# Moving the statistics of chunks three and four into the feed-forward loop of an audio tower on one core

## The reference

```python
h = tok(x)                                              # projection, dynamic convolution, feed-forward, residual
h = h + attn(layernorm(h), w_qkv, b_qkv, w_o, b_o)      # out = vals @ w_o.T + b_o
h = h + ffn(layernorm(h), up, down, perm)
```

## Time and profile before

| what | value |
|---|---|
| median of 3 runs | 1031.34 us |
| time of the profiled execution | 1035.96 us |
| its span, first to last instruction | 1034.2 us |
| mean granted TensorE clock | 0.977 of full |
| PE busy | 967.4 us (94%) |
| DVE, ACT, POOL busy | 509.2, 424.4, 394.3 us |
| DMA, mean over the span | 121 GB/s |

### The profile page before, as it was taken

How to read it: one execution, slowest core, us unless ns; L and a number is a source line. 1 busy time by engine, 2 the same in 40 slices (tenths; PEclk the granted TensorE clock), 3 DMA queues, 4 the chain that set the end, 5 groups by cost and what they waited for, 6 DMA issues and landing times.

```text
span 1034.2 us, 15644 instructions
## 1 busy us (share of the span) xinstructions
PE 967.4 (94%) x6108; PEld 714.5 (69%) x6108; DVE 509.2 (49%) x848; ACT 424.4 (41%) x753; POOL 394.3 (38%) x317
## 2 busy tenths in 40 slices
PE   7999999987899999999879999999999999889996
PEld 5777777776777788778657877877887777323331
DVE  6153535659447502254756256256064567755551
ACT  6144444555433533434243243243132332356553
POOL 1225252227601122723361451451023377748532
PEclk9999999999899999999989999999999999899998
DMA  8542725395343154327100201200214975533421
GB/s 290 209 165 4 205 7 181 4 285 203 117 145 107 62 126 164 109 95 265 41 11 22 92 11 35 79 11 22 92 52 149 289 260 209 184 111 133 149 77 61
DMA packets 75062, 124.96 MB, mean 121 GB/s; under 512 B 29159, under 2 KB 38375, under 8 KB 70894
## 3 DMA queue, kind: packets, MB, share of 16 engines
q1 hardware_dynamic: 68830, 107.03, 33.7%
q0 software_dynamic: 5120, 16.78, 4.6%
q10 hardware_dynamic: 1040, 0.16, 0.1%
HBM read 81.46 MB, written 42.50 MB: 120 GB/s over the span
## 4 chain that ended last, share of the span: by engine, by line
PE 53%; issue 10%; POOL 7%; DVE 5%; DMA 3%; ACT 2%; another core or an unknown queue 1%; POOLq 0%; SPq 0%; DVEq 0%; ACTq 0%
PE bank L299 14%; PE bank L301 13%; PE bank L300 13%; PE bank L1795 3%; PE bank L1804 3%; POOL vacc L335 2%; PE bank L1551 1%; POOL out L758 1%; POOL acc L363 1%; DVE sq L377 1%; DMA stage<-w_qkv_t 1%; POOL acc L308 1%; DVE acc L1219 1%; PE bank L1523 1%; DMA db_late<-h_s 1%
## 5 line engine op out<-in xcount | busy, mean ns | idle before, releaser
L335 POOL TENSOR_TENSOR vacc<-vacc,sq 128x512 f32<-128x512 f32 x72 | 97.2, 1350 | 45.8 <-ACT sq L381 36.4
L299 PE MATMUL bank<-xa_h,wp_h 128*128 128x512 f32 x256 | 103.4, 404 | 7.2 <-DVE xa_l L1094 7.2
L299 PE MATMUL bank<-cv_h,wf_h 128*128 128x512 f32 x256 | 106.3, 415 | 1.2 <-POOL wf_l L293 1.2
L301 PE MATMUL bank<-cv_h,wf_l 128*128 128x512 f32 x256 | 101.4, 396 | 0.0
L300 PE MATMUL bank<-cv_l,wf_h 128*128 128x512 f32 x256 | 101.4, 396 | 0.0
L300 PE MATMUL bank<-xa_l,wp_h 128*128 128x512 f32 x256 | 101.1, 395 | 0.0
L301 PE MATMUL bank<-xa_h,wp_l 128*128 128x512 f32 x256 | 101.1, 395 | 0.0
L700 POOL TENSOR_TENSOR fo<-fo,res 128x512 f32<-128x512 f32 x32 | 43.5, 1373 | 123.4 <-ACT fo L837 89.8
L1077 ACT ACTIVATE gt<-bank 128x512 f32<-128x512 f32 x128 | 66.2, 600 | 39.0 <-PE bank L1795 36.8
L1795 PE MATMUL bank<-dd,up_f 64*128 64x512 f32 x256 | 67.9, 651 | 5.6 <-ACT gt L1077 5.4
L381 ACT ACTIVATE sq<-sq 128x512 f32<-128x512 f32 x56 | 35.1, 632 | 79.3 <-DVE sq L377 79.3
(11 more groups left out here) (179 smaller groups left out, 2167.5 us busy)
## 6 DMA issues: line engine op xcount, KB each, us to landing
xs<-x_t SPq DMA_DIRECT2D x32, 256.0 KB, 6.2
h_s<-ho SPq DMA_DIRECT2D x8, 1024.0 KB, 5.9
res<-h_s SPq DMA_DIRECT2D x32, 256.0 KB, 3.6
h_s<-fo SPq DMA_DIRECT2D x32, 256.0 KB, 2.4
dc<-h_s SPq DMA_DIRECT2D x4, 2048.0 KB, 9.3
h<-h_s SPq DMA_DIRECT2D x8, 1024.0 KB, 10.5
h_s<-h SPq DMA_DIRECT2D x8, 1024.0 KB, 4.8
stage<-w_qkv_t SPq DMA_DIRECT2D x24, 256.0 KB, 3.6
```

Source lines behind the costliest of these rows:

```text
L299: pe.matmul(o, wh, xh, start=start, stop=False)
L301: return pe.matmul(o, wl, xh, start=False, stop=stop)
L335: g.tensor_tensor(vacc[:, :], t[:, 0, :] if k == 1 else vacc[:, :], t[:, k % 2, :], ALU.add).then_inc(ln_pool, 1)
```

## The change

The centres, squares, adds and the variance product of chunk three (number 2) leave the output projection of chunk four and go into the feed-forward loop: its centres into steps 0 to 3, two a step, its variance product behind step 5, its root behind the gelus of step 6. Those of chunk four go into steps 7 to 12 (one, two, one, two, one, one), its variance product behind step 14. The mean product of chunk four moves from step 1 to step 5, its copy from step 2 to step 6. Both variance products now write into bank 7. In the last output-projection chunk DVE runs `d_prep` of chunk one's blocks 0 to 3, moves banks 0 to 2 out, runs `d_prep` of blocks 4 to 7, and goes on with the other banks. `d_prep` of the later chunks starts at step 4 and not 3. In every projection chunk `o_sum` now stands ahead of the last low-part split of the next chunk. SP stores chunk three's reciprocal after `d_stat_load(1)`. The one counter `ln_pool` (14 a statistic) is split into `ln_sum` and `ln_vac` (7 each), so that sums and adds of different chunks can interleave; this renames waits and changes no count that they stand for (the hunks with renames alone are left out).

```diff
@@ -169,8 +169,8 @@
-        ln_pool, ln_mean, ln_d, ln_sq, ln_var, ln_std, ln_rstd = (
-            sem(s) for s in ("ln_pool", "ln_mean", "ln_d", "ln_sq", "ln_var", "ln_std", "ln_rstd"))
+        ln_sum, ln_vac, ln_mean, ln_d, ln_sq, ln_var, ln_std, ln_rstd = (
+            sem(s) for s in ("ln_sum", "ln_vac", "ln_mean", "ln_d", "ln_sq", "ln_var", "ln_std", "ln_rstd"))
...
@@ -638,12 +638,13 @@
                                  h2[c % 2][:, 4 * g:4 * g + 4, :]).then_inc(o_st[c % 2][g], 16)
                 if c > 0 and c + 1 < CH:
                     h2_load(c + 1)
-                if c > 0:
+                if 0 < c < CH - 1:
                     stat_store(CH + c - 2, 1)
                 if c == 1:
                     d_stat_load(0)
 
             d_stat_load(1)
+            stat_store(2 * CH - 3, 1)
             d_stat_load(2)
             stat_store(2 * CH - 2, 0)
             stat_store(2 * CH - 2, 1)
@@ -766,14 +767,16 @@
                     gather(0, range(4))
                 if c == 3:
                     gather(0, range(4, KB))
-                ln_var_pool(g, 2 * CH + c - 1)
+                if c < CH - 1:
+                    ln_var_pool(g, 2 * CH + c - 1)
                 o_sum(c)
 
             gather(1)
             for s in range(CH * KB + 1):
-                k = s - STAT_FROM
-                if 0 < k < KB:
-                    ln_var_add(g, 3 * CH - 1, k)
+                for i, steps in enumerate(CENTERS):
+                    for k in steps.get(s - 1, ()):
+                        if k > 0:
+                            ln_var_add(g, 3 * CH - 2 + i, k)
                 if s > 0:
                     scatter((s - 1) // KB, (s - 1) % KB)
                 n, k = divmod(s - GATHER_AFTER, KB)
@@ -1059,11 +1062,11 @@
                     if c == 1:
                         act.wait_ge(vo_st, 64 * CH)
                     stat_copy_act(act, L, CH + c - 2)
-                    for k in range(KB):
+                    for k in range(KB if c < CH - 1 else 0):
                         stat_square_act(act, L, k)
                 if c + 1 < CH:
                     vs_high(c + 1, range(PAIRS - 1))
-                if c > 0:
+                if 0 < c < CH - 1:
                     stat_std_act(act, L, VAR_BANK)
                 if c + 1 < CH:
                     vs_high(c + 1, [PAIRS - 1])
@@ -1079,12 +1082,14 @@
             L = 3 * CH - 1
             for s in range(CH * KB):
                 gelus(s // KB, s % KB)
-                if s == 2:
+                for i, steps in enumerate(CENTERS):
+                    for k in steps.get(s, ()):
+                        stat_square_act(act, L - 1 + i, k)
+                if s == VAR_AT[0] + 1:
+                    stat_std_act(act, L - 1, FF_VAR_BANK)
                     stat_copy_act(act, L, 2 * CH - 2)
-                if 0 <= s - STAT_FROM < KB:
-                    stat_square_act(act, L, s - STAT_FROM)
-                if s == STAT_FROM + KB:
-                    stat_std_act(act, L)
+                if s == VAR_AT[1] + 1:
+                    stat_std_act(act, L, FF_VAR_BANK)
 
 
         @block.vector
...
@@ -1384,20 +1389,22 @@
                 v.tensor_tensor(dd[:, k, :], dd[:, k, :], rtd[n % 2][:, :], ALU.mult).then_inc(xd_sc, 1)
 
             for c in range(CH):
-                if c > 0:
+                if 0 < c < CH - 1:
                     o_center(c - 1, range(4))
+                if c == CH - 1:
+                    d_prep(0, range(4))
                 o_evac(c, A_GROUPS[0])
-                for k in range(4, KB) if c > 0 else ():
-                    o_center(c - 1, [k])
-                    if c == CH - 1:
-                        d_prep(0, [k - 4])
+                if 0 < c < CH - 1:
+                    o_center(c - 1, range(4, KB))
+                if c == CH - 1:
+                    d_prep(0, range(4, KB))
                 o_evac(c, A_GROUPS[1])
                 if c + 1 < CH:
                     o_low(c + 1, range(PAIRS - 1))
                 o_evac(c, A_GROUPS[2])
+                o_sum(c)
                 if c + 1 < CH:
                     o_low(c + 1, [PAIRS - 1])
-                o_sum(c)
                 if 0 < c < CH - 1:
                     stat_recip_dve(v, 2 * CH + c - 1)
 
@@ -1414,13 +1421,10 @@
                 n, k = divmod(s - PREP_AFTER, KB)
                 if 0 <= n < CH - 1:
                     d_prep(n + 1, [k])
-                d_prep(0, LAST_PREP.get(s, ()))
-                if s == 0:
-                    stat_recip_dve(v, 3 * CH - 2)
-                if 0 <= s - STAT_FROM < KB:
-                    o_center(CH - 1, [s - STAT_FROM])
-                if s == STAT_FROM + KB:
-                    stat_recip_dve(v, 3 * CH - 1)
+                for i, steps in enumerate(CENTERS):
+                    o_center(CH - 2 + i, steps.get(s, ()))
+                    if s == VAR_AT[i] + 2:
+                        stat_recip_dve(v, 3 * CH - 2 + i)
             d_add(CH - 1, KB - 1)
 
         @block.tensor
@@ -1779,7 +1783,7 @@
                         if c > 0 and (g, k) == (0, 2):
                             pe.wait_ge(o_ev, 8 * c)
                             stat_mean_pe(pe, 2 * CH + c - 1)
-                        if c > 0 and (g, k) == (2, 3):
+                        if 0 < c < CH - 1 and (g, k) == (2, 3):
                             pe.wait_ge(o_ev, 8 * c + VAR_BANK + 1)
                             stat_var_pe(pe, 2 * CH + c - 1, CH + c - 2, VAR_BANK)
 
@@ -1808,8 +1812,6 @@
             pe.wait_ge(up_ld, 32)
             pe.wait_ge(dn_ld, 64)
             for blk in range(2):
-                if blk == VAR_BANK // 2:
-                    pe.wait_ge(ln_std, 3 * CH - 1)
                 ff_up(0, 0, blk)
             pe.wait_ge(o_ev, 8 * CH)
             for s in range(CH * KB):
@@ -1819,10 +1821,11 @@
                         ff_up((s + 1) // KB, (s + 1) % KB, blk)
                 for i in range(FFB):
                     ff_down(c, a, i)
-                if s == 1:
+                for i in range(2):
+                    if s == VAR_AT[i]:
+                        stat_var_pe(pe, 3 * CH - 2 + i, 2 * CH - 3 + i, FF_VAR_BANK)
+                if s == VAR_AT[0]:
                     stat_mean_pe(pe, 3 * CH - 1)
-                if s == STAT_FROM + KB - 1:
-                    stat_var_pe(pe, 3 * CH - 1, 2 * CH - 2)
 
 
 
@@ -1838,9 +1841,11 @@
 
 VAR_BANK = 3
 
-LAST_PREP = {0: (4, 5), 1: (6, 7)}
-
-PREP_AFTER, STAT_FROM, GATHER_AFTER = 3, 5, 4
+CENTERS = ({0: (0, 1), 1: (2, 3), 2: (4, 5), 3: (6, 7)},
+           {7: (0,), 8: (1, 2), 9: (3,), 10: (4, 5), 11: (6,), 12: (7,)})
+VAR_AT, FF_VAR_BANK = (5, 14), 7
+
+PREP_AFTER, GATHER_AFTER = 4, 4
 
 
 def cv_banks(n, h):
```

More of the change, by code:

```diff
@@ L304, in ln_sum_pool @@
         def ln_sum_pool(g, L, blk):
-            g.tensor_tensor(acc[:, :], blk(0), blk(1), ALU.add).then_inc(ln_pool, 1)
+            g.tensor_tensor(acc[:, :], blk(0), blk(1), ALU.add).then_inc(ln_sum, 1)
             for k in range(2, KB):
-                since(g, ln_pool, L, 14, k - 1)
-                g.tensor_tensor(acc[:, :], acc[:, :], blk(k), ALU.add).then_inc(ln_pool, 1)
+                since(g, ln_sum, L, 7, k - 1)
+                g.tensor_tensor(acc[:, :], acc[:, :], blk(k), ALU.add).then_inc(ln_sum, 1)
         def ln_mean_pe(pe, L):
-            since(pe, ln_pool, L, 14, 7)
+            since(pe, ln_sum, L, 7, 7)
             since(pe, ln_std, L - 1, 1, 1)
@@ L322, in ln_square_act @@
             if k >= 2:
-                since(act, ln_pool, L, 14, 7 + max(1, k - 2))
+                since(act, ln_vac, L, 7, max(1, k - 2))
             act.activation(squares(L)[:, k % 2, :], d, ACT.Square).then_inc(ln_sq, 1)
@@ L332, in ln_var_add @@
             if k > 1:
-                since(g, ln_pool, L, 14, 7 + k - 1)
+                since(g, ln_vac, L, 7, k - 1)
             t = squares(L)
             g.tensor_tensor(vacc[:, :], t[:, 0, :] if k == 1 else vacc[:, :], t[:, k % 2, :],
-                            ALU.add).then_inc(ln_pool, 1)
+                            ALU.add).then_inc(ln_vac, 1)
         def ln_var_pool(g, L):
@@ L342, in ln_var_pe @@
         def ln_var_pe(pe, L):
-            since(pe, ln_pool, L, 14, 14)
+            since(pe, ln_vac, L, 7, 7)
             since(pe, ln_d, L, 8, 8)
@@ L361, in stat_sum_pool @@
             if k > 1:
-                since(g, ln_pool, L, 14, k - 1)
-            g.tensor_tensor(acc[:, :], blk(0) if k == 1 else acc[:, :], blk(k), ALU.add).then_inc(ln_pool, 1)
+                since(g, ln_sum, L, 7, k - 1)
+            g.tensor_tensor(acc[:, :], blk(0) if k == 1 else acc[:, :], blk(k), ALU.add).then_inc(ln_sum, 1)
         def stat_copy_act(act, L, S):
@@ L375, in stat_center @@
             if k >= 2:
-                since(e, ln_pool, L, 14, 7 + max(1, k - 2))
+                since(e, ln_vac, L, 7, max(1, k - 2))
             e.tensor_tensor(sq[:, k % 2, :], src, mean_t[:, :], ALU.subtract).then_inc(ln_d, 1)
@@ L922, in b_step @@
```

(10 more changed lines are left out.)

## The result

In five runs the changed kernel took 1038.34 us in the median (1036.77 to 1042.3), the kernel before 1030.89 us (1030.0 to 1031.8) beside it. The ratio is 1.0072, with a 95% interval of 1.0054 to 1.009: 7.4 us slower. The forecast was 1035.4 and slower. The time lies in the stated range of 1029 to 1039, but above the band of 1033.5 to 1037.5 that the prediction gave to its forecast by itself.

What follows compares the result with a forecast made beforehand. PE's idle and slow clock between the last projection product and D(31) bound the kernel; terms of 20.8 us excess after, against 16.8 in timed runs before, add 4.0 to 1031.34, giving 1035.4 us, range 1029 to 1039.

Steps and rivals of the forecast that it cites:

- start, U(0) to U(2): First loop steps: U(1) and U(2) wait for the first gelus, 0.5 and 0.6 us, 1.1 in all.
- pause before U(3), clock: Block 1's add waits behind POOL's eight gathers, so PE idles 4.6 us, then loses 1.6 to a lower clock.
- behind step 5: Variance product 1.96 us and mean product 1.06, both on PE's path in the loop: 3.0 us.
- step 8, with the 0.75 before it, clock: Two centres in one step, the add behind a scatter and gather, delay U(10): 3.7 us plus 1.4 of clock.
- steps 9 to 13: POOL's six adds in four steps need 18.8 us against 15.1; 3.4 us lost after what step 8's pause covers.
- behind step 14: Chunk four's variance product in PE's loop: 1.96 us without clock loss, 3.6 with it; 2.0 in the sum.
- excess: Time from last projection product to D(31) beyond the ideal 121.1 us; 20.8 forecast after, 16.8 assumed for timed runs before.
- Handover: Boundary from projection to loop: U(0) starts directly behind the last projection product; the move gives 7.5 us.
- rival 3: DVE and POOL collide: three added adds meet chain instructions at 1.1 us each, 3.3 us, giving 1038.7; chance 0.13.
- the profile's disturbance: PE's signals reached DVE and ACT late near 900 to 907, costing 4.6 us; assumed absent from timed runs.
- 1: Rival: late signals belong to every execution and the change removes what provokes them; 1030.7 us, chance 0.25.
- 2: Rival: the gathers don't hold the chain, so the 6.2 us before U(3) are not lost; 1029.2 us, chance 0.12.

Runs made afterwards that it cites:

- e2: Changed kernel with chunk two's eight gathers laced into steps 0 to 5 instead of ahead of POOL's loop; ratio to the kernel before 1.0013.
- e3: Changed kernel with chunk four's centres one a step in steps 7 to 14, variance product behind step 15; ratio to the kernel before 0.9987.
- e4: Changed kernel with both chunk two's gathers laced into steps 0 to 5 and chunk four's centres one a step; ratio to the kernel before 0.9969.
- e6: Changed kernel with laced gathers, chunk four's centres one a step, and each centre ahead of d_add and d_prep on DVE; ratio to the kernel before 0.9988.
- e1: Kernel before, no edit, profiled once more; 1030.81 us.
- e12: Kernel before, no edit, a third profile; 1031.7 us.
- e8: Kernel before with SP issuing the two broadcast loads of chunk three's statistics six prepared blocks later; ratio to the kernel before 1.0004.
- e5: Changed kernel again, no edit, on another run's chip beside the kernel before; ratio to the kernel before 1.0061.

## Why the prediction was right

By its steps, on the changed kernel's trace (each stretch is start to start, less 1.92 for a U and 1.87 for a D in it):

| step | predicted us | measured us |
|---|---|---|
| start, U(0) to U(2) | 1.1 | 0.5 (882.98 to 889.20) |
| pause before U(3), clock | 4.6 + 1.6 | 5.16 + 2.6 |
| behind step 5 | 3.0 | 2.9 |
| step 8, with the 0.75 before it, clock | 3.7 + 1.4 | 3.6 + 1.6 |
| steps 9 to 13 | 3.4 | 2.9 |
| behind step 14 | 2.0 | 2.0 |
| excess | 20.8 | 21.3 |

- *Handover*: right. U(0) starts behind the last projection product.
- *The pause before U(3)*: right. The gathers began at 883.83 and the add stood behind them until 893.82; I had 882.9 and 893.0. What was short is the clock: a pause of 5.16 us was followed by slow products over U(3) and D(2), 1.8 + 0.8 us, where I took the 1.6 of U(14).
- *Steps 0 to 3 and step 8*: e2 took out the first pause and e3 the second, by the order of instructions alone, and e4 both. The mechanism is shown.
- *Steps 9 to 13*: the size was near, the reason half wrong. I put it down to POOL's 4.06 us a step. e6 has all of POOL's work there and no pause, so it is the chain through DVE (d_add, two prep instructions, centre), in which prep instructions were at times longer while POOL was adding (rival 3 below).
- *The kernel before*: the timed runs don't have the profile's disturbance as a rule, as I took it, but the reason I gave, an accident of one execution, is not quite it: it came in two of three, at a price of 0.7 to 4.6 us. Its excess is 15.2 us undisturbed, and 16.1 with e1's late signals, and not 16.8, mostly because the variance product's 1.6 us of clock came in one profile of three. That term, with the 0.5 by which the changed kernel's excess is above the sum, makes the difference 5.2 to 6.1 us by the traces and not 4.0; the times say 6.3 to 7.4, intervals 4.0 to 9.3. What may be left, about 1 us, is not settled. It is not in the projection (101.3 and 101.4 us in the two traces of the changed kernel) and not behind D(31); the start of the projection, ahead of which the code is alike, scatters by more.
- *Rivals*: 1 falls. The late signals don't belong to every execution (e12 has none), and with them e1 took 1030.81 us and without them e12 1031.7; e8, which has none, is no faster (1.0004). 2 falls: each gather had its pitch of 1.25 or more. 3, the port, holds in part. The longer instructions are there (0.94, 1.05, 1.11, 1.45 and twice 1.64 us for prep instructions of 0.68, 3.7 us of DVE in all, and the same ones in e5), and three of them stand in the chain for which U(13) and U(14) waited, the 0.94 at 943.86 and these two:

```profile
944.83 1.64 DVE L1389 TENSOR_TENSOR dd<-dd,rtd 128x512 f32<-128x512 f32 x1
...
949.03 1.45 DVE L1382 TENSOR_TENSOR dd<-hg,mtd 128x512 f32<-128x512 f32 x1
```

With 0.68 each, U(14) would start about 0.8 us earlier: an estimate from these rows, against the 3.3 of the rival. The others cost PE nothing. With chunk four's centres one a step (e3), one of 0.94 is left in these steps, so some of e3's 4.7 us may be the port's. And place decides, not length: in e6 six prep instructions between 938 and 961 us took 2.06 to 2.19 us each, behind the centre and so outside the chain, and PE has no pause there.
- *The number*: that 1038.34 lies so near the 1038.7 of rival 3, and the 1038.6 for both variance products with a clock loss, is chance. The port made 0.8 us, and neither variance product of the changed kernel pulled the clock down. The forecast was 2.9 us too low, and the largest known part of that is that it took the kernel before's excess 1.6 us too high. The range held the time by bounds that had been drawn for other causes.

## What to carry to other kernels

When a step is moved into a loop, follow its waits through every queue it passes, not the engines' busy shares: in the changed loop's first 79 us (883 to 962) POOL was busy for 70%, ACT for 59%, DVE for 52%, and yet two adds that stood behind transfers' issue on POOL held up PE by way of DVE and ACT for 5.2 and 2.7 us. Put a short instruction that others wait for ahead of long issues that nobody waits for yet, and don't let one step of a loop hold both ends of a dependence that goes through another engine's queue. The move itself was sound: with the gathers laced in and chunk four's centres one a step it is 0.3% faster than before. Busy shares count once the order is right: with every centre alone in its step, POOL was busy for 86% from 903 to 929 us, and PE lost 2.4 us to it.

## What the runs showed of the hardware

- In two of three executions of the same kernel, DVE and ACT instructions that wait for PE started 1.8 to 4.3 us later than the third execution's lags give: ACT's gelu 5.49 us behind the start of U(3) and not 1.17, DVE's d_add 3.81 and 3.83 behind the start of D(2) and not 2.01. PE lost 4.6 and 0.7 us by it. In none of eleven executions with two broadcast loads fewer beside the gathers did it happen; the cause stays open.
- Whether products are slow behind eight one-column products of 2.0 us is not fixed by the code: behind the last of them in the kernel before, U took 3.60 us in one execution and 1.99 in two.
- A pause of PE didn't settle the clock by its length alone. Before U(10), pauses of 2.72 us (changed kernel) and 2.25 us (e2, with another of 1.22 before U(9)) were followed by slow products, U(10) taking 3.47 and 2.99 us; before U(4) and U(5) in e6, pauses of 2.67 and 3.16 us were followed by 2.01.
- The eight gathers ahead of the loop took 0.94 to 1.09 us of POOL each, one every 1.25 to 1.4 us, and held up the add behind them for 10.0 us (883.83 to 893.82).
